# A context attention that follows a self-attention, spread over the last output projection and the first steps of its MLP

## The reference, cut to what matters

```python
x = _layernorm(x + _L0_attn_ref(x, ...))    # 16 heads of 64; z @ w_o; returns x + z
x = _layernorm(x + _L0_xattn_ref(x, ctx_1024, ...))
# _L0_xattn_ref, one head of 256, 64 context rows for each batch:
kv = _kv @ W_kv + b_kv;  k, v = jnp.split(kv, 2, axis=-1);  q = _q @ W_q + b_q
attn = jax.nn.softmax(jnp.einsum('bqh,bkh->bqk', q, k), axis=-1)
out = jnp.einsum('bqk,bkh->bqh', attn, v)
hidden = jax.nn.gelu(out @ W1 + b1);  return hidden @ W2 + b2
```

## Time and profile before

| | |
|---|---|
| median of 3 runs | 2615.37 us (2611.33 to 2617.66) |
| the profiled execution's own time | 2624.42 us |
| its span | 2622.6 us |
| PE busy | 2396.0 us (91%) |
| DVE, ACT, POOL busy | 1670.5, 1253.8, 896.7 us |
| mean granted clock of PE | 0.962 |

### The profile page before, as it was taken

How to read it: one execution, slowest core, us unless ns; L and a number is a source line. 1 busy time by engine, 2 the same in 40 slices (tenths; PEclk the granted TensorE clock), 3 DMA queues, 4 the chain that set the end, 5 groups by cost and what they waited for, 6 DMA issues and landing times.

```text
span 2622.6 us, 35270 instructions
## 1 busy us (share of the span) xinstructions
PE 2396.0 (91%) x13518; PEld 1715.5 (65%) x13520; DVE 1670.5 (64%) x3036; ACT 1253.8 (48%) x1967; POOL 896.7 (34%) x474
## 2 busy tenths in 40 slices
PE   8999999999999889899999999998899999995662
PEld 7555556755555569788888889897566566554521
DVE  5666755566765445877443443445788888878967
ACT  4565554355555144344444444443266655552442
POOL 3776776277777250202210220301220000303323
PEclk9999999999999899899999999999899999997985
DMA  2000001001000120001100110000434433310000
GB/s 78 13 20 18 13 13 45 13 13 25 13 21 17 47 75 1 33 1 33 33 14 21 33 41 1 9 1 1 107 83 96 95 78 79 88 36 5 1 1 32
DMA packets 57431, 88.08 MB, mean 34 GB/s; under 512 B 13992, under 2 KB 37808, under 8 KB 57264
## 3 DMA queue, kind: packets, MB, share of 16 engines
q1 hardware_dynamic: 56992, 85.70, 12.5%
q10 hardware_dynamic: 272, 0.13, 0.0%
HBM read 37.16 MB, written 2.10 MB: 15 GB/s over the span
## 4 chain that ended last, share of the span: by engine, by line
PE 75%; DVE 13%; ACT 4%; issue 3%; POOL 3%; DMA 1%; SPq 1%; ACTq 0%; DVEq 0%; POOLq 0%
PE PS L85 74%; DVE m_gl L1106 2%; DVE s_nm L1562 2%; ACT a_P L533 2%; POOL a_sum L683 2%; ACT a_QS L482 1%; DVE X L273 1%; DVE st_s L234 1%; DVE x_rd L1985 1%; POOL f_H L2193 1%; DVE x_E L2000 1%; DVE x_sm L2005 0%; DVE s_T L1539 0%; DVE st_r L260 0%; PE PS L2044 0%
## 5 line engine op out<-in xcount | busy, mean ns | idle before, releaser
L1106 DVE TENSOR_TENSOR m_gl<-m_g,m_gh 128x512 fp32r<-128x512 f32 x288 | 258.1, 902 | 386.5 <-ACT m_g L945 386.5
L683 POOL TENSOR_TENSOR a_sum<-a_sum,a_P 128x1024 f32<-128x1024 f32 x192 | 456.3, 2376 | 69.3 <-ACT a_P L533 45.3
L533 ACT ACTIVATE a_P<-PS 128x512 f32<-128x512 f32 x512 | 293.4, 600 | 278.7 <-PE PS L85 261.0
L942 ACT ACTIVATE m_gh<-PS,cols 128x512 fp32r<-128x512 f32 x288 | 198.4, 689 | 470.0 <-PE PS L85 470.0
L578 DVE TENSOR_REDUCE a_nm<-PS 128x1 f32<-128x1024 f32 x256 | 301.6, 1217 | 131.4 <-PE PS L85 129.6
L1562 DVE TENSOR_REDUCE s_nm<-PS 128x1 f32<-128x512 f32 x512 | 331.3, 683 | 77.1 <-PE PS L85 74.1
L85 PE MATMUL PS<-m_w2h,m_gh 128*128 128x256 f32 x1152 | 324.9, 282 | 18.8 <-DVE m_gl L1106 18.6
L85 PE MATMUL PS<-m_w2l,m_gh 128*128 128x256 f32 x1152 | 323.4, 281 | 0.0
L85 PE MATMUL PS<-m_w2h,m_gl 128*128 128x256 f32 x1152 | 323.2, 281 | 0.0
L1460 ACT ACTIVATE s_P<-PS 128x1024 f32<-128x1024 f32 x256 | 248.1, 1022 | 107.7 <-PE PS L85 107.3
L85 PEld LDWEIGHTS PS<-m_w2h,m_gh 128*128 128x128 f32 x1152 | 218.2, 189 | 35.2 <-DVE m_gl L1106 23.6
(11 more groups left out here) (288 smaller groups left out, 4174.3 us busy)
## 6 DMA issues: line engine op xcount, KB each, us to landing
m_raw<-in_m_w SPq DMA_DIRECT2D x16, 1024.0 KB, 5.1
s_Q<-s_T SPq DMA_DIRECT2D x128, 128.0 KB, 2.4
s_K<-s_T SPq DMA_DIRECT2D x128, 128.0 KB, 2.4
a_KH<-a_KH SPq DMA_DIRECT2D x64, 128.0 KB, 2.4
a_wr<-in_w_qk SPq DMA_DIRECT2D x16, 256.0 KB, 2.8
X<-in_x SPq DMA_DIRECT2D x4, 512.0 KB, 6.3
a_P<-in_w_v SPq DMA_DIRECT2D x8, 256.0 KB, 5.9
m_raw<-in_c_w SPq DMA_DIRECT2D x2, 1024.0 KB, 8.6
```

Of the source, the lines that this page charges most:

```text
L533: e.activation(a_P[:, g % N_P, half * 512:half * 512 + 512], PS[:, s0 + half, :], ACT.Exp).then_inc(s["a_exp"], 1)
L683: e.tensor_tensor(o[:, :], a_P[:, (g - 1) % N_P, :] if k == 1 else o[:, :], a_P[:, g % N_P, :], ALU.add).then_inc(s["a_add"], 1)
L942: e.activation(m_gh[r][:, :], PS[:, 4 + n % 3, :], func, bias=cols[:, bcol:bcol + 1]).then_inc(s["m_gh"], 1)
L1106: e.tensor_tensor(m_gl[r][:, :], m_g0[r][:, :], m_gh[r][:, :].bitcast(F32), ALU.subtract).then_inc(s["m_gl"], 1)
```

## The change

The context attention is cut into functions (`context_tokens`, `context_keys`, `context_query`, `context_scores`, `context_softmax`, `context_turned`, `context_out`) that are called for one batch or group at a time.

Batch 0: its four token steps run on PE right after the last weighing matmuls of the self-attention, ahead of `totals`; keys and values, four queries and the scores are set between the tiles of `project_last`; its softmax lies between DVE's additions of the last tiles; its transposes and `out` matmuls stand at the head of `pe_rest`, and on DVE the second norm's 25 instructions are dealt out in sevens between them. Batch 1: a table `EARLY` names for each of the steps 0 to 12 what runs at that step's end. The loads follow the last a_sum addition rather than the norm; the split of the query weights moves from DVE to POOL, ahead of `split(0)`; some tiles get other places in SBUF. The plan of the later steps is as it was.

```diff
+            def project_last():
+                e.wait_ge(s["a_wo"], 32)
...
+                e.wait_ge(s["t_xl"], 12)
+                e.wait_ge(s["a_nz"], 30)
+                for j in range(4):
+                    out_tile(1, j, range(7))
+                context_keys(e)
+                e.wait_ge(s["a_nz"], 31)
+                for j in range(4):
+                    out_tile(1, j, (7,))
+                e.wait_ge(s["a_nz"], 32)
+                for j in range(4, 8):
+                    e.wait_ge(s["a_yd"], 8 + j - 3)
+                    out_tile(1, j, range(8))
+                    if j == 4:
+                        for i, bk in enumerate((0, 1, 6, 0)):
...
+                            context_query(e, i // 2, i % 2, bk)
+                    if j == 5:
+                        e.wait_ge(s["c_vd"], 1)
+                        context_scores(e, 0, 7)
@@ pe_l0, after the last weigh
+                else:
+                    e.wait_ge(s["normed"], 8)
+                    for i in range(4):
+                        if i >= 2:
+                            e.wait_ge(s["t_xl"], 8 + i - 1)
+                        context_tokens(e, i, 4 + i % 2)
@@ dve_l0, at its end
-            project(1)
+            e.wait_ge(s["rows"], 16)
+            e.wait_ge(s["c_kv"], 2)
+            e.tensor_tensor(c_v[:, :], PS[:, 7, 0:256], rows[:, 0, :], ALU.add).then_inc(s["c_vd"], 1)
+            for j in range(8, 12):
+                out_tile(1, j)
+            pump([norm(8)], 99)
+            softmax = context_softmax(e, own, 0, 7)
+            for j in range(12, 16):
+                out_tile(1, j)
+                if j in (13, 14):
+                    pump([softmax], 2 if j == 13 else 3)
+            slow = [norm(12)]
+            for g in range(2):
+                for m in range(2):
+                    pump(slow, 7)
+                    context_out_low(e, g, m, 2 + m)
@@ sp_l0, at its end
+            e.wait_ge(s["a_pv"], 2 * N_G)
+            e.wait_ge(s["a_add"], 224)
+            e.dma_start(c_wkv[:, :, :], A["c_wkv"].rearrange(kp, p=128)).then_inc(s["c_l1"], 16)
+            e.dma_start(c_ct[:, :, :], A["ctxT"].rearrange(kp, p=128)).then_inc(s["c_l1"], 16)
+            e.dma_start(c_wq[:, :, :], A["c_wq"].rearrange(kp, p=128)).then_inc(s["c_l0"], 16)
...
@@ before pe_rest
+        EARLY = {0: [("tokens", 4, 7), ("tokens", 5, 2)], 1: [("tokens", 6, 3), ("tokens", 7, 7)],
+                 2: [("query", 2, 0, 2), ("query", 2, 1, 3)], 3: [("query", 3, 0, 7), ("query", 3, 1, 2)],
+                 5: [("scores", 1, 3)], 8: [("turned", 2, 7)], 9: [("out", 2, 0, 7)], 10: [("out", 2, 1, 7)],
+                 11: [("turned", 3, 0)], 12: [("out", 3, 0, 1), ("out", 3, 1, 7)]}
...
+        def pe_rest(e):
+            for g in range(2):
+                context_turned(e, g, g)
+            for g in range(2):
+                for m in range(2):
+                    if g:
+                        e.wait_ge(s["c_ol"], m + 1)
+                    else:
+                        e.wait_ge(s["a_yd"], 13 + m)
+                    context_out(e, g, m, 2 + m)
+            e.wait_ge(s["a_yd"], 16)
@@ pe_rest, in each step n behind its matmuls (act_rest and dve_rest likewise)
+                for what in EARLY.get(n, []):
+                    early(what)
@@ act_rest
+                if n == 6:
+                    context_exp(e, 1)
@@ dve_rest
-            e.wait_ge(s["c_l0"], 16)
-            e.tensor_copy(c_wqh[:, :, :], c_wq[:, :, :]).then_inc(s["c_wqs"], 1)
-            e.wait_ge(s["c_wqs"], 1)
-            e.tensor_tensor(c_wql[:, :, :], c_wq[:, :, :], c_wqh[:, :, :].bitcast(F32), ALU.subtract).then_inc(s["c_wqs"], 1)
...
+                if n == 7:
+                    pump([softmax], 3)
@@ pool_rest
-            e.wait_ge(s["normed"], 16)
+            e.wait_ge(s["c_l0"], 16)
+            e.tensor_copy(c_wqh[:, :, :], c_wq[:, :, :]).then_inc(s["c_wqs"], 1)
...
+                elif k:
+                    e.wait_ge(s["a_y"], 16)
+                else:
+                    e.wait_ge(s["a_dn"], 32)
@@ sp_rest
-            e.wait_ge(s["normed"], 16)
-            e.dma_start(rows[:, :, :], A["rows"].partition_broadcast(128)).then_inc(s["rows"], 16)
...
```

More of the change, by code:

```diff
@@ new lines, in context_exp, with context_turned @@
+        def context_exp(e, b):
+            e8 = c_E[:, 8 * b:8 * b + 8, 64 * b:64 * b + 64]
+            e.wait_ge(s["c_sub"], b + 1)
+            e.activation(e8, e8, ACT.Exp).then_inc(s["c_exp"], 1)
+        def context_turned(e, g, bk):
+            e.wait_ge(s["c_E"], g // 2 + 1)
+            e.wait_ge(s["c_e0"], g // 2 + 1)
+            for q in range(4):
+                t = e.transpose(PS[:, bk, q * 128:(q + 1) * 128], c_E[:, 4 * g + q, :], ident[:, :])
+            t.then_inc(s["c_et"], 1)
@@ new lines, in act_rest, with early @@
+            context_exp(e, 0)
+            for g in range(2):
+                context_turned_out(e, g, g)
+            for g in range(2):
+                for m in range(2):
+                    context_out_high(e, g, m, 2 + m)
+            def early(what):
+                if what[0] == "tokens":
+                    context_tokens_high(e, what[1], what[2])
+                elif what[0] == "query":
+                    context_query_out(e, what[1], what[2], what[3])
+                elif what[0] == "turned":
+                    context_turned_out(e, what[1], what[2])
+                elif what[0] == "out":
+                    context_out_high(e, what[1], what[2], what[3])
@@ L1077, in dve_rest, with early @@
-            for g in range(4):
-                for m in range(2):
-                    cs = slice(g * 512, g * 512 + 512)
-                    e.wait_ge(s["c_oh"], 2 * g + m + 1)
-                    e.tensor_tensor(xl[:, m, cs], PS[:, 2 + m, :], xh[:, m, cs].bitcast(F32), ALU.subtract).then_inc(s["c_ol"], 1)
+            softmax = context_softmax(e, own, 1, 3)
+            def early(what):
+                if what[0] == "tokens":
+                    context_tokens_low(e, what[1], what[2])
+                elif what[0] == "scores":
+                    pump([softmax], 2)
+                elif what[0] == "out":
+                    context_out_low(e, what[1], what[2], what[3])
```

311 lines of the change are left out of this document (164 added, 147 removed).

## The result

| | before | changed |
|---|---|---|
| median | 2616.51 us (4 runs, 2611.33 to 2619.83) | 2591.35 us (4 runs, 2588.14 to 2593.94) |
| profiled execution, own time | 2624.42 us | 2590.35 us |
| its span | 2622.6 us | 2588.6 us |
| mean granted clock | 0.962 | 0.966 |

What follows compares the result with a forecast made beforehand. PE bounds the kernel, with idle or low-clock time between projection and MLP. The MLP starts 39.8 us earlier, less 16.0 us of moved work and 2.1 us of waits: 21.7 us less, median 2615.4 to 2593.7 us, range 2587 to 2606.

Steps and rivals of the forecast that it cites:

- The start: Wait for POOL's additions before the totals: four token steps go in at 0.1 us cost, projection starts at 872.8 us.
- So I take no gain: At the totals: token steps would not raise the 0.50 clock, gain 0; the other end was 2.7 us.
- the clock stays up: Rival at the totals and projection: token steps keep the clock up, 2.7 us more gain, 2591.0 us; chance 0.12.
- The projection: Projection with batch 0's keys, values, queries and scores inside: 39.5 us of PE, ending at 912.3 us, nothing late.
- The tail: Serial piece between projection and MLP: 6.5 us and 0.3 us of handovers, MLP starting at 919.1 us.
- The MLP's first steps: Steps 0 to 12 take on batch 1's pieces: 16.0 us of PE work plus 2.1 us of waits.
- The two waits: PE waits 0.7 us in step 1 for the last token step and 1.4 us in step 8 for batch 1's softmax.
- `split(1)` at 0: POOL's split falling on MLP steps 3 to 8 was priced at 0, with bounds 0 and 8.7 us.
- the port holds DVE: Rival in MLP steps 3 to 8: split(1) costs 8.7 us, 13.0 us less in all, 2602.4 us; chance 0.20.
- Out of overlap: Rival in the MLP's 13 early steps: each exposes ACT and DVE passes, 12.6 us slower, 2628.0 us; chance 0.03.

Runs made afterwards that it cites:

- w_late: Changed kernel with the loads of the MLP's own weights held until 12 tiles are normed; 2592.14 us (one run).
- b1_first_clear: Changed kernel with all of batch 1 ahead of MLP step 0, and split(1) waiting for the MLP's first second-layer group; 2611.15 us (one run).
- split1_late: Changed kernel with split(1) held until twelve slices of the MLP are through their second layer; 2595.92 us (one run).
- split1_tail: Changed kernel with split(1) ahead of POOL's bias additions to tiles 8 to 15; 2600.11 us (one run).
- b1_first: Changed kernel with the whole of batch 1 ahead of step 0 of the MLP; 2609.52 us (10 runs), ratio 0.9974 to the kernel before.

## Why the prediction was right, point by point

**The start: right in the work, wrong on the clock.** "So I take no gain" is the sentence that failed. I took the stretch from 912 to 914 us, in which transposes ran at 0.50, for evidence that transposes would not keep the clock up in the wait either. That stretch showed a clock that was already down. The profile after has 1.00 throughout; the totals took 1.94 us, and P to the first projection matmul 2.14 us where I had 3.9. The ends of the range that I had kept for this step were 0 and 2.7 us, and the measured gain is the upper end: 1.7 us at the start and 0.9 in the projection. The rival "the clock stays up", with a chance of 0.12, was what happened, and the median of 2591.35 us lies nearer to its 2591.0 than to my 2593.7. The Trainium skill ("TensorE: Matmul & The Clock Gate", Part 4, PE-mode transpose) says of transpose mode that it doesn't count as PE being busy in the same way; by that rule the wait would have ended at 0.50 as before. All twelve profiles with token steps in the wait disagree (totals of 1.94 us in each), and the two with an empty wait show 0.50 and 3.68 us, so the measurement decides. That the token steps in the wait keep the clock up is shown; whether it is their work that counts or the shorter unbroken idle time (2.69 us at most, against 3.7), no run separates.

**The projection: right.** 38.9 us (868.15 to 907.06) against 39.5. Keys and values took 2.0 us where I had 1.6, the 64 projection matmuls 27.7 where I had 28.6, again by the clock. No gap, and none of the margins was used up: `split(0)` ended at 890.2 us, 23 us ahead of M. `w_late` shows that the margin that counts is smaller, the 15 us up to the softmax's multiply at 905.1 us: a subtraction beside that one costs 3.1 us before the weights themselves are late. The forecast had overlooked one hold here: beside POOL the norm of tiles 8 to 11 took 13.2 us (884.7 to 897.9) instead of 5.8; it cost nothing, PE had no gap.

**The tail: right,** 6.3 us against 6.8, at full clock and with three short handovers.

Together P to M came out at 47.4 us where the sum had 50.2: 2.8 us, nearly all by the clock. With the 1.2 us of the next part they are the 4.0 us by which the trace's 25.7 exceed the forecast's 21.7.

**The MLP's first steps: right.** 16.9 us against 16.0 + 2.1 = 18.1. The two waits stood where they were put, 0.52 and 1.20 us against 0.7 and 1.4. The pieces themselves took 15.1 us, 0.9 less than their sum. Against the same steps before, steps 2 and 3 grew by 5.1 us by their queries where I had 5.6, and steps 8 to 12 by 4.3 us without the wait, where I had 4.9 for the transposed groups and four `out` at 1.0; step 10, with a single `out` and nothing else to it, is 0.9 us longer than a plain one.

**`split(1)` at 0: right, and shown.** The rival "the port holds DVE" (chance 0.20, 2602.4 us) had its mechanism right and its price wrong. Two `m_gl` were held, the first until 0.56 us behind the end of POOL's subtraction. The Trainium skill ("SBUF — State Buffer", on the shared port pair) has it that a DVE instruction with two SBUF inputs and a GpSimd one that reads SBUF exclude each other for the whole of the one that starts first, and the row agrees. A held `m_gl` is wanted two steps later, and those steps are stretched by the queries and scores; both halves of this reason are needed, since in `b1_first_clear` the same split beside plain steps left PE idle and cost 2.7 us. `split1_late` took the split away and found nothing; `split1_tail` and `b1_first` show the price where the result is wanted at once.

**Out of overlap: did not happen.** PE was idle 1.7 us of 50.7 in the thirteen steps.

What my sum held without a price of its own is the second effect of the old order: behind serial handovers the clock was lowered, and it was low for the matmuls that followed. I worked the tail and the steps out from work at full clock, so it was in the result, but I missed it in the expectations: three of them (batch 1 first, batch 0 behind the projection, `split(1)` in the tail) came out too small by 2.5 to 9.4 us, and each time the profile shows a stretch at 0.50.

## What to carry to other kernels

A serial chain between engines costs twice, by PE's idle time and by the lowered clock of the matmuls behind it: where it can't be shortened, cut it into pieces and set each between dense matmuls at a distance of a step or more from its use. Put any small piece of PE work into a wait that is left; two token steps in a wait of 3.7 us gave back 1.7 us of totals here. GpSimd's long subtractions belong beside DVE work whose result is wanted late, and beside no softmax or norm that PE waits for: the same split cost 0, 2.7, 3.4 or 10 us by its place.

## What the runs showed of the hardware that I had not expected

- Transposes in a wait kept the granted clock at 1.00 (twelve profiles), even with 2.69 us of idle time between them and the totals; with the wait empty for 3.69 us it was 0.50.
- The granted clock fell to 0.50 for some 3 us while the profile shows PE without a gap, behind the router's narrow matmuls, and in other versions with the same work there it stayed at 1.00. Such a step is 1.5 us of difference between two versions that their edits don't explain.
- A DVE instruction on 128x4 numbers with its input in SBUF is held by POOL as well as a large one. In the kernel with the query weights on DVE, the first waits for a long subtraction, and the next takes 0.66 us instead of 0.17 beside POOL's eight additions of 0.70 us each; in `split1_tail` a cast held one for 1.80 us (rows of DVE, then of POOL):

```profile
886.84 3.91 DVE L245 TENSOR_SCALAR st_r<-st_a 128x4 f32<-128x4 f32 x1
890.79 0.66 DVE L249 TENSOR_SCALAR st_r<-st_r 128x4 int32<-128x4 int32 x1
```

```profile
886.15 4.58 POOL L1313 TENSOR_TENSOR m_w2l<-m_raw,m_w2h 128x2048 fp32r<-128x2048 f32 x1
890.68 5.57 POOL L1320 TENSOR_TENSOR X<-X,rows 128x256 f32<-128x256 f32 x8
```
